# A graph layer's gathers through a circle of 8 pairs of row tiles in place of 35

## The chip, the cores and the metric

The kernel runs on one core of one Trainium2 chip. The metric is the device time of one execution in microseconds (us). TensorE is PE, VectorE is DVE, ScalarE is ACT, GpSimd is POOL, and SP is the engine that issues most of the plain DMAs. PE's weight loads are listed apart, as PEld.

## The reference

There are N = 3125 nodes with 128 features and 50000 edges, sorted by destination `dst`. Each edge has one of 16 types, each node one of 8.

```python
h   = relu(layernorm(x))
hW  = einsum('nd,tdf->tnf', h, W_edge) + b_edge[:, None, :]
msg = hW[etypes, src] / counts[dst, etypes]          # mean over the edges of one type at one node
agg = segment_sum(msg, dst)
hN  = einsum('nd,tdf->tnf', h, W_node) + b_node[:, None, :]
out = x + relu(hN[ntypes, arange(N)] + agg)
```

## The kernel before

The kernel first makes h for all nodes, splits it in two float16 halves and stores them as `h_table` in HBM, 25 blocks of 128 nodes. The edge weights are applied late: the kernel first sums h[src] over the edges of each (node, type), and then multiplies these sums by `W_edge`.

The 50000 edges are 391 tiles of 128, taken in 196 pairs of tiles (`PAIRS`). For each tile POOL issues one indirect DMA (line 390), the gather, which fetches the 128 rows h[src] from `h_table` into one slot of `G`. The second tile of every eighth pair is not gathered: PE makes it from the h that lies in SBUF with one-hot products (`pe_fetch`, line 276), and ACT puts it into `G` (line 283). So there are 368 gathers, 15 for each 8 pairs.

PE's `sums` takes a pair's two slots and multiplies them by one-hots of (type, destination) that DVE writes into `oh` (line 964): four matmuls of line 693, at whose end it raises `pair_mm`. DVE then adds the result into `S` (line 973). Each group of 8 pairs (`PPB`) completes one block of 128 nodes: DVE scales the sums by reciprocal counts (`dve_scale`, line 353), SP loads the next block's 1 MB of reciprocals (line 247), ACT zeroes (line 309), and PE multiplies by the weights of nodes and edges between its next pairs (lines 328 to 337).

POOL's order is its program. It issues the 6 gathers of the first three pairs (`LATE`), reads a flag, waits for `mask_ready`, which DVE raises after line 907, and then goes through the pairs. Ahead of each gather stands a wait that the gather three before it has landed (`NEAR`), and ahead of each pair from the 36th on a wait for `pair_mm`: the pair 35 before it must have been summed, since `G` is a circle of `BODY + LATE` = 35 pairs. The first 25 slots of `G` hold, until line 907 has read them, `nt_row`, the types of the nodes; that is why the wait for `mask_ready` stands there.

Before its sums, PE counts the edges of each (node, type) with 392 small matmuls (line 673), in turns with DVE (line 931) and ACT (line 592). Between its sixth and seventh pair it waits for a one-hot of DVE, which at that time joins the counts and takes their reciprocals (lines 990 to 998).

Of the kernel before, what the change touches and what calls it, by code (L numbers as in the profile page):

```python
# [25 lines left out]
def gnn_layer(nc, x, src, dst, etype, ntype, w_edge, b_edge, w_node, b_node, out):  # L26
# [18 lines left out]
    LATE = 3  # L45
    NEAR = 3
    BODY = 4 * PPB
    ITERS = (PAIRS - LATE) // BODY
    assert PAIRS - LATE - ITERS * BODY == 1 and NB == 4 * ITERS + 1 and R * W <= 512
    AHEAD = 128  # L50
    TURN = 8
    H_SCALE = 4096.0
    MID = NB * P // 2
# [19 lines left out]
    with ctx:  # L73
        def sb(name, shape, dt):
            return ctx.enter_context(nc.sbuf_tensor(name, shape, dt))
# [4 lines left out]
        def sem(name):  # L80
            return ctx.enter_context(nc.semaphore(name))
# [20 lines left out]
        src_t = sb("src_t", [P, TC], I32)  # L102
# [97 lines left out]
        mask_ready = sem("mask_ready")  # L200
# [8 lines left out]
        issuing = sem("issuing")  # L209
        landed = [sem(f"landed{m}") for m in range(TURN)]  # L210
        oh_ready = sem("oh_ready")
        pair_mm = sem("pair_mm")
# [68 lines left out]
        def act_fetch(act, b):  # L281
            act.wait_ge(fetch_mm, b + 2)
            nc.scalar.activation(G[:, 2 * slot_of(LATE + PPB * b + PPB - 1) + 1, :], misc[:, 0:2 * D],  # L283
                                 ACT.Copy).then_inc(fetched, 1)
# [88 lines left out]
            return got  # L373

        def slot_of(pair):
            return (pair + BODY) % (BODY + LATE)

        def is_fetched(pair, a):
            return a == 1 and pair != PAIRS - 1 and pair >= LATE and (pair - LATE) % PPB == PPB - 1

        def gathers_upto(pair, a):

            return 2 * pair + a - sum(is_fetched(p, 1) for p in range(pair))

        def wait_landed(engine, n):

            engine.wait_ge(landed[n % TURN], 16 * (n // TURN + 1))

        def gather(pool, slot, index, done):
            nc.gpsimd.indirect_dma_start(  # L390
                out=G[:, slot, :], out_offset=None, in_=h_table[:, :],
                in_offset=bass.IndirectOffsetOnAxis(ap=index, axis=0)).then_inc(done, 16)
# [67 lines left out]
        @block.gpsimd  # L460
        def _(pool):
            nc.gpsimd.memset(ones[:, :], 1.0)
            nc.gpsimd.memset(zcol[:, :], 0.0)
            nc.gpsimd.memset(id32[:, :], 0.0).then_inc(consts, 1)
            nc.gpsimd.memset(bias[:, :], 0.0).then_inc(consts, 1)
            pool.wait_ge(consts, 1)
            nc.gpsimd.affine_select(out=id32[:, :], in_=id32[:, :], compare_op=ALU.not_equal, fill=1.0,
                                    base=0, pattern=[[-1, P]], channel_multiplier=1).then_inc(consts, 1)
            pool.wait_ge(consts, 3)
            nc.gpsimd.tensor_copy(id16[:, :], id32[:, :]).then_inc(consts, 1)  # L470
            with nc.allow_low_precision(reason="integers up to 2048 are exact in float16"):
                nc.gpsimd.iota(iota[:, :], pattern=[[1, R * P + 1]], base=0, channel_multiplier=0,
                               allow_small_or_imprecise_dtypes=True)
            nc.gpsimd.iota(pair16[:, :], pattern=[[16, PAIRS]], base=0, channel_multiplier=0,
                           allow_small_or_imprecise_dtypes=True).then_inc(consts, 1)
            pool.wait_ge(consts, 5)
            nc.gpsimd.iota(kcol[32:64, :], pattern=[[0, 1]], base=0, channel_multiplier=1,
                           allow_small_or_imprecise_dtypes=True).then_inc(consts, 1)
            pool.wait_ge(consts, 6)
            nc.gpsimd.iota(node_col[:, :], pattern=[[P, NB]], base=-MID, channel_multiplier=1,  # L480
                           allow_small_or_imprecise_dtypes=True)
            nc.gpsimd.memset(S[:, :, :], 0.0).then_inc(zeroed_s, 1)
            nc.gpsimd.memset(bsel[0:64, :], 0.0).then_inc(zeroed_s, 1)

            pool.wait_ge(src_ready, 1)
            pool.wait_ge(h_stored, 16 * 5)
            for j in range(LATE):
                for a in range(2):
                    gather(pool, 2 * (BODY + j) + a, src_t[:, 2 * j + a:2 * j + a + 1],
                           landed[2 * j + a])  # L490
            pool.wait_ge(flag_ready, 1)
            bad = pool.value_load(flag[0:1, 0:1], min_val=0, max_val=FLAG_MAX)
            pool.wait_ge(mask_ready, 1)
            with pool.If(bad < 1):
                for n in range(2 * LATE - NEAR):
                    wait_landed(pool, n)
                for pair in range(LATE, PAIRS):
                    if pair >= LATE + BODY:

                        pool.wait_ge(pair_mm, pair - LATE + 1)  # L500
                    for a in range(2):
                        if not is_fetched(pair, a):
                            n = gathers_upto(pair, a)
                            wait_landed(pool, n - NEAR)
                            pool.sem_inc(issuing, 1)  # L505
                            gather(pool, 2 * slot_of(pair) + a, src_t[:, 2 * pair + a:2 * pair + a + 1], landed[n % TURN])
            with pool.Else():
                for s in range(0, NB, SEG):
                    with pool.Fori(0, min(SEG, NB - s) * NT) as n:
                        pool.wait_ge(g_src, s * NT + n + 1)  # L510
                        pool.sem_inc(issuing, 1)
                        gather(pool, 0, src_s[:, 0:1], g_rows[s // SEG])
                        pool.wait_ge(g_rows[s // SEG], (n + 1) * 16)
# [122 lines left out]
        def _(pe):  # L636
# [24 lines left out]
            with pe.If(bad < 1):  # L661
# [37 lines left out]
                for j in range(LATE):  # L699
                    if j == 2:  # L700
                        pe.wait_ge(c_out, 2 * CITERS + 1)
                    sums(j, j, slot_of(j), (j - LATE) % 4, 0)
# [65 lines left out]
        def _(dve):  # L768
# [108 lines left out]
            def in_range(cols, values, low, high):  # L877

                own(nc.vector.tensor_scalar(viol[:, cols], values, -0.5 * (low + high), 2.0 / (high - low + 1),
                                            ALU.add, ALU.mult))  # L880
            in_range(slice(0, V1 // 2), rel[:, 0:V1:2], 0, W0 - 1)
            in_range(slice(V1 // 2, V1), rel[:, 1:V1:2], 0, W - 1)
            in_range(slice(V1, V2), relq[:, :], 0, WQ - 1)
            in_range(slice(V2, V3), viol[:, V2:V3], -16 * LATE, AHEAD)
            in_range(slice(V3, V4), viol[:, V3:V4], WQ, 2 * N)
# [229 lines left out]
```

## Time and profile before

| what | value |
|---|---|
| median of 3 runs | 623.2 us (619.66 to 623.7) |
| time of the profiled execution | 623.44 us |
| its span in the trace | 621.5 us |
| mean granted clock of PE | 0.857 of full speed |
| gathers, their busy time on POOL | 368, 392.2 us |
| POOL idle just before a gather, in total | 198.3 us |

The span runs from the first instruction to the last; the profiled execution took 1.9 us more than its span. A gather's row on POOL is the making of its descriptors; its data land some us later.

### The profile page before, as it was taken

What the parts mean: (1) busy time and instruction counts of PE and PEld (TensorE: products, weight loads), DVE (VectorE), ACT (ScalarE), POOL (GpSimd) and SP (SyncE); (2) the same over time, 40 slices, a digit from 0 to 9 for tenths busy, and PEclk for the clock granted to TensorE, in tenths of its full rate; (3) what the DMA queues carried; (4) which work ended last, traced back from release to release, by engine and by line L of the source; (5) the groups of instructions that cost most, each with busy time, mean ns of one, the idle gap of its engine ahead of it and who ended that gap; (6) DMA issues with size and microseconds to landing.
All of it is one profiled execution on the core that took longest, in us unless ns stands there. A gap on an engine that the chain in (4) does not pass through costs nothing.

```text
span 621.5 us, 9756 instructions
## 1 busy us (share of the span) xinstructions
PE 434.3 (70%) x3143; PEld 351.9 (57%) x3143; DVE 363.0 (58%) x913; ACT 172.7 (28%) x402; POOL 405.8 (65%) x384
## 2 busy tenths in 40 slices
PE   0269849977786675776776776767766776776687
PEld 0169628865565563665564565555645564565477
DVE  5966778876635545645645545646545646545633
ACT  2922424423313303213203213213203203303300
POOL 8067775666765576766766765766766766776760
PEclk9755559997977977978987978988898978988979
DMA  5541154333323313223323223223223323323320
GB/s 149 147 108 51 38 165 163 120 117 111 111 64 112 114 51 104 74 91 119 91 80 109 78 89 114 81 90 111 87 83 112 90 81 112 104 64 116 112 55 13
DMA packets 32497, 60.35 MB, mean 97 GB/s; under 512 B 7416, under 2 KB 22836, under 8 KB 29236
## 3 DMA queue, kind: packets, MB, share of 16 engines
q1 hardware_dynamic: 19372, 34.83, 17.1%
q0 software_dynamic: 11776, 24.14, 14.2%
q10 hardware_dynamic: 1296, 0.71, 0.5%
q8 instruction: 28, 0.46, 0.3%
q14 instruction: 25, 0.20, 0.1%
HBM read 56.01 MB, written 3.65 MB: 96 GB/s over the span
## 4 chain that ended last, share of the span: by engine, by line
DMA 57%; issue 17%; PE 16%; POOL 6%; DVE 2%; ACT 1%; SPq 1%; POOLq 0%; DVEq 0%; ACTq 0%
DMA G<-h_table,src_t 56%; POOL G L390 6%; PE out_ps L337 6%; PE acc L693 5%; PE misc L276 2%; PE out_ps L328 1%; DMA xs<-in_x_dram 1%; ACT union_a L543 1%; SPq L402 1%; PE misc L337 1%; PE node_ps L317 0%; POOLq L505 0%; PE out_ps L330 0%; DVE bsel L907 0%; PE misc L328 0%
## 5 line engine op out<-in xcount | busy, mean ns | idle before, releaser
L390 POOL DMA_INDIRECT G<-h_table,src_t x368 | 392.2, 1066 | 198.3 <-DMA G<-h_table,src_t 113.6
L693 PE MATMUL acc<-oh,G 128*128 128x384 f16 (+1 forms) x784 | 148.7, 322 | 150.6 <-issue 83.5
L973 DVE TENSOR_TENSOR S<-S,acc 128x384 f32 x196 | 108.2, 552 | 207.5 <-PE acc L693 207.0
L693 PEld LDWEIGHTS acc<-oh,G 128*128 128x128 f16 x784 | 75.3, 105 | 214.1 <-issue 124.2
L337 PE MATMUL out_ps<-w_all,union_a 128*128 128x128 f32 x768 | 120.7, 324 | 0.0
L337 PEld LDWEIGHTS out_ps<-w_all,union_a 128*128 128x128 f32 x768 | 116.7, 240 | 0.8
L964 DVE TENSOR_SCALAR oh<-iota,seg 128x224 f16<-128x224 f16 (+1 forms) x396 | 102.7, 313 | 10.3 <-issue 10.3
L283 ACT ACTIVATE G<-misc 128x256 f16<-128x256 f32 x24 | 9.2, 384 | 317.4 <-PE misc L276 306.7
L276 PE MATMUL misc<-hh,union_c 128*128 128x256 f16 x600 | 79.5, 278 | 0.0
L276 PEld LDWEIGHTS misc<-hh,union_c 128*128 128x128 f16 x600 | 59.7, 100 | 6.2
L296 ACT ACTIVATE dg<-id,wmask 128x128 f16<-128x128 f16 x200 | 60.7, 386 | 0.0
L309 ACT ACTIVATE S<-zcol 128x2048 f32<-128x2048 f32 x23 | 43.9, 1909 | 59.1 <-DVE union_a L353 59.1
L353 DVE TENSOR_TENSOR union_a<-S,union_b 128x2048 f32<-128x2048 f32 (+1 forms) x25 | 56.1, 2243 | 0.9
L267 DVE TENSOR_TENSOR union_c<-src_r,union_d 128x1024 f16<-128x1024 f16 (+1 forms) x72 | 50.9, 707 | 2.5
L328 PE MATMUL out_ps<-w_all,hN 128*128 128x128 f32 x384 | 49.5, 284 | 0.0
L328 PEld LDWEIGHTS out_ps<-w_all,hN 128*128 128x128 f32 x384 | 47.3, 201 | 0.1
L673 PE MATMUL acc<-union_c 128*16 128x44 f16 x392 | 31.0, 256 | 6.9 <-DVE union_c L931 6.9
L673 PEld LDWEIGHTS acc<-union_c 128*16 128x16 f16 x392 | 30.8, 114 | 7.0 <-DVE union_c L931 7.0
L317 PE MATMUL node_ps<-dg,hh 128*128 128x512 f16 x100 | 27.1, 395 | 0.0
L304 ACT ACTIVATE hN<-node_ps 128x1024 f32<-128x1024 f32 x25 | 25.0, 1001 | 0.0
L641 PE MATMUL acc<-id,union_b 128*128 128x128 f32 x12 | 2.8, 423 | 17.1 <-DVE union_b L837 17.1
L317 PEld LDWEIGHTS node_ps<-dg,hh 128*128 128x128 f16 x100 | 10.2, 102 | 7.3 <-issue 1.1
(97 smaller groups left out, 171.1 us busy)
## 6 DMA issues: line engine op xcount, KB each, us to landing
union_b<-rc_table SPq DMA_DIRECT2D x25, 1024.0 KB, 4.8
G<-h_table,src_t POOLq DMA_INDIRECT x368, 2.6
h_table<-hh SPq DMA_DIRECT2D x5, 320.0 KB, 2.6
src_row<-in_src_dram SPq DMA_DIRECT2D x24, 64.0 KB, 2.9
out_dram<-os SPq DMA_DIRECT2D x24, 64.0 KB
xs<-in_x_dram SPq DMA_DIRECT2D x4, 320.0 KB, 5.1
w_all<-in_L_gnn_W_node_dram SPq DMA_DIRECT2D x1, 512.0 KB
xs<-in_x_dram SPq DMA_DIRECT2D x1, 256.0 KB
```

Of the source, the lines that this page charges most:

```text
L267: nc.vector.tensor_tensor(fetch[:, first:end, :], src_r16[:, p:p + 1, :].to_broadcast([P, end - first, P]), node_of[:, first:end, :], ALU. ...
L276: last = nc.tensor.matmul(misc[:, 0:2 * D], fetch[:, k, :], hh[:, k, :], start=(k == 0), stop=(k == NB - 1))
L296: last = nc.scalar.activation(dg[:, p, k, :], id16[:, :], ACT.Copy, scale=wmask[:, bass.ds(b, 1), k])
L309: nc.scalar.activation(S[:, :, r * P:(r + 1) * P], zeros3, ACT.Copy).then_inc(zeroed, 1)
L328: nc.tensor.matmul(into[0:rows, 0:D], hN[:, p, k, 0:rows], w_all[:, R + k, :], start=(k == 0), stop=False)
L337: last = nc.tensor.matmul(into[0:rows, 0:D], Sn[:, p, t, 0:rows], w_all[:, t, :], start=False, stop=(t == R - 1))
L353: nc.vector.tensor_tensor(Sn[:, p, :, 0:rows], S[:, :, r * P:r * P + rows], rcb[:, p, :, 0:rows], ALU.mult).then_inc(scaled, 1)
L390: nc.gpsimd.indirect_dma_start(out=G[:, slot, :], out_offset=None, in_=h_table[:, :], in_offset=bass.IndirectOffsetOnAxis(ap=index, axis=0 ...
L673: last = nc.tensor.matmul(bank[0:R, v * WQ:(v + 1) * WQ], tcnt[:, q, :, 4 * v + a], ncnt[:, q, :, 4 * v + a], start=(a == 0), stop=(a == 3))
L693: last = nc.tensor.matmul(window[:, :, 0:w], G[:, 2 * g_slot + a, part * D:(part + 1) * D], oh[:, o, a, 0:R * w].rearrange("p (t n) -> p t ...
L964: last = nc.vector.tensor_scalar(oh[:, o, a, 0:width], iota_w[:, 0:width], cols[:, a:a + 1], None, ALU.is_equal)
L973: nc.vector.tensor_tensor(span, span, acc[bank][:, 0:R * W].rearrange("p (t n) -> p t n", n=W), ALU.add).then_inc(s_add, 1)
```

## The change

`slot_of` puts the pairs into a circle of 8 (`SLOTS`), the last 8 of the 35 pairs of slots. POOL therefore waits, from the ninth pair on, until the pair 8 before it has been summed. Those slots don't overlap `nt_row`, and the wait for `mask_ready` moves into the other path (`Else`), which these inputs don't take. `G` keeps its size; the gathers, their order and the waits on landings stay.

```diff
+    SLOTS = 8
...
         def slot_of(pair):
-            return (pair + BODY) % (BODY + LATE)
+            return BODY + LATE - SLOTS + pair % SLOTS
...
-                    gather(pool, 2 * (BODY + j) + a, src_t[:, 2 * j + a:2 * j + a + 1],
+                    gather(pool, 2 * slot_of(j) + a, src_t[:, 2 * j + a:2 * j + a + 1],
                            landed[2 * j + a])
...
-            pool.wait_ge(mask_ready, 1)
             with pool.If(bad < 1):
...
-                    if pair >= LATE + BODY:
+                    if pair >= SLOTS:
-                        pool.wait_ge(pair_mm, pair - LATE + 1)
+                        pool.wait_ge(pair_mm, BODY + pair - SLOTS + 1)
...
             with pool.Else():
+                pool.wait_ge(mask_ready, 1)
```

(`pair_mm` starts at `BODY`, so both waits ask for a number of sums: pair - 34 and pair - 7.)

## Rows read from the trace of the kernel before

**Rows 1.** The page: the chain that ended last, by engine.
```profile
DMA 57%; issue 17%; PE 16%; POOL 6%; DVE 2%; ACT 1%; SPq 1%; POOLq 0%; DVEq 0%; ACTq 0%
```

**Rows 2.** Waits of PE, first 69 to 130 us, then 130 to 605: total, times, longest.
```profile
PE acc L693 <- DVE oh L964: 11.4, 2, 10.3
...
PE acc L693 <- issue: 83.5, 62, 4.4
PE acc L693 <- DMA G<-h_table,src_t: 55.3, 19, 6.1
```

**Rows 3.** Gathers on POOL in six stretches: busy (x gathers), PE clock, DMA share, GB/s.
```profile
30.00:54.90 24.90, 17.67 (x16) 0.50 0.37 98
54.90:70.60 15.70, 10.81 (x11) 0.50 0.19 49
70.60:87.60 17.00, 13.86 (x10) 0.60 0.30 71
87.60:128.40 40.80, 25.76 (x23) 0.94 0.48 161
128.40:587.60 459.20, 312.19 (x296) 0.88 0.30 94
587.60:605.00 17.40, 11.94 (x12) 0.80 0.33 110
```

**Rows 4.** Timeline of POOL, single gathers: start, duration, idle before and its releaser.
```profile
38.26 0.94 POOL L390 DMA_INDIRECT G<-h_table,src_t  x1 [0.30 <-issue]
40.69 0.94 POOL L390 DMA_INDIRECT G<-h_table,src_t  x1 [1.49 <-DMA G<-h_table,src_t]
...
53.38 1.30 POOL L390 DMA_INDIRECT G<-h_table,src_t  x1 [0.30 <-issue]
54.98 0.94 POOL L390 DMA_INDIRECT G<-h_table,src_t  x1 [0.30 <-issue]
...
65.60 0.94 POOL L390 DMA_INDIRECT G<-h_table,src_t  x1 [1.81 <-DMA G<-h_table,src_t]
...
70.65 0.95 POOL L390 DMA_INDIRECT G<-h_table,src_t  x1 [0.30 <-DMA G<-h_table,src_t]
...
73.16 5.36 POOL L390 DMA_INDIRECT G<-h_table,src_t  x1 [0.30 <-DMA G<-h_table,src_t]
...
604.03 0.95 POOL L390 DMA_INDIRECT G<-h_table,src_t  x1 [0.30 <-issue]
```

**Rows 5.** Timeline of PE, 69 to 91 us (a pair is four matmuls of L693).
```profile
69.27 3.20 PE L693 MATMUL acc<-oh,G 128*128 128x384 f16 x12 [1.11 <-DVE oh L964]
...
73.97 2.27 PE L693 MATMUL acc<-oh,G 128*128 128x384 f16 x12
86.51 2.19 PE L693 MATMUL acc<-oh,G 128*128 128x384 f16 x8 [10.28 <-DVE oh L964]
...
90.41 1.22 PE L693 MATMUL acc<-oh,G 128*128 128x384 f16 x4
```

**Rows 6.** Timeline of DVE: mask input, add of the first pair, joining the counts.
```profile
32.21 1.88 DVE L907 TENSOR_SCALAR bsel<-G,kcol 8x3200 f32<-8x3200 int32 x1
...
70.57 0.55 DVE L973 TENSOR_TENSOR S<-S,acc 128x384 f32 x1
...
73.07 3.47 DVE L990 TENSOR_TENSOR union_b<-union_b,union_a 16x3200 f32<-16x3200 f32 x1
76.58 1.81 DVE L993 TENSOR_SCALAR bsel<-union_b 16x3200 f32<-16x3200 f32 x1
```

**Rows 7.** Timeline of PE, the same place in two groups of 8 pairs.
```profile
98.26 1.21 PE L693 MATMUL acc<-oh,G 128*128 128x384 f16 x8
...
111.91 1.21 PE L693 MATMUL acc<-oh,G 128*128 128x384 f16 x8
```

**Rows 8.** Waits of POOL, 130 to 605 us.
```profile
POOL G L390 <- DMA G<-h_table,src_t: 96.9, 146, 3.7
POOL G L390 <- issue: 49.2, 152, 2.5
POOL G L390 <- PE acc L693: 6.3, 9, 2.4
```

**Rows 9.** The page: gathers, median us from issue to landing.
```profile
G<-h_table,src_t POOLq DMA_INDIRECT x368, 2.6
```

## The prediction

> **What bounds the kernel now.** I read the chain that ended last first: 57% of it is DMA, nearly all of it the landing of gathers, and PE has 16% [rows 1]. That names the gathers, but not whether their data or their issue sets the pace, nor from when. The waits of PE answer when: from 69 to 130 us it waits only for one-hots of DVE, 11.4 us in all; from 130 to 605 us its waits are for landed gathers, 55.3 us, and for something that the profile can't name, 83.5 us, and none for DVE [rows 2]. So PE begins with rows to spare and has used them up by about 130 us.
>
> Next the pace of POOL, as gathers in stretches [rows 3]. By 128.4 us it has issued 16 + 11 + 10 + 23 = 60 of 368; then 296 more take 459.2 us, 1.551 us each, or 23.3 us for the 15 of a group. Undisturbed, two gathers start 1.25 us apart: 0.94 us of work and 0.30 us between [rows 4]. Fifteen would take 18.75 us, so each group carries 4.5 us of disturbance: gathers stretched while DVE scales a block, and waits for the landing of the third gather before while the 1 MB of reciprocals come in. The waits of POOL have the size of it [rows 8]. PE alone does 8 pairs with all work between them in 111.91 - 98.26 = 13.65 us [rows 7]. POOL needs 23.3 us for what PE does in 13.65 us: the string of gathers, begun at about 30 us and ended at 604.03 us [rows 3, 4], is the bound, and what follows it, to the span's end at 621.5 us, is a fixed tail of 17.5 us. PE's head start in rows is spent by 130 us and never comes back. Hence the rule for the sum: any us that POOL stands still before its last gather is a us at the end, unless that us would have been lost to POOL anyway.
>
> **The new wait.** Pairs 1 to 8 have 16 gathers, and POOL has issued these 16 by 54.9 us: the 16th starts at 53.38 [rows 3, 4]. The 17th started at 54.98. With 8 pairs of slots it needs the sum of the first pair. PE begins that at 69.27 us and does three pairs in 3.20 us [rows 5]; DVE, which waits for the same signal, starts its add at 70.57 [rows 6]. With the usual step between signal and gather, POOL resumes at about 70.8. Nothing in the change brings PE forward here: it is counting until then, in turns with DVE and ACT, and uses no gathered row. The stall is 70.8 - 54.98 = 15.8 us. Queued behind the waiting instruction on POOL are all 352 gathers that are left; for them waits PE.
>
> **What the stall swallows.** The 11 gathers that POOL made in 54.9 to 70.6 us [rows 3] now come after it. There they had taken 70.65 - 54.98 = 15.67 us, 1.92 us above 11 x 1.25 = 13.75, chiefly the idle 1.81 in place of 0.30 before the gather at 65.60 [rows 4]. What disturbs the string later is tied to blocks (scaling, reciprocals), of which there are as many as before; so the 11 are priced bare, at 13.75 us. Resuming at 70.8 one place where 27 gathers stood at 70.65: +0.15. Together +13.9 us.
>
> **Is there a second stall?** From 70.8 on, each pair asks for the one 8 before it. Sums of pairs 1 to 6 are over by 76.24 us, pair 7 begins at 86.51 [rows 5]. POOL now makes the 11 gathers of pairs 9 to 14. One of them will fall on DVE's joining of counts (73.07 to 78.4) and be held as that at 73.16 was, 5.36 us in place of 0.94 [rows 4, 6]. The 11 so end at 70.8 + 13.75 + 4.4 = 88.95 us, and then pair 15 asks for pair 7, over at about 87.7 [rows 5]: no wait. If the gather weren't held, POOL would be there at 84.5 and wait until 88.0: 0.9 us sooner than with the hold, no more. So either way the string stands at 88 to 89 us with 27 gathers issued, where it stood at 87.6 with 37 [rows 3]. Check: 10 gathers are missing, 12.5 us, and 1.3 us of clock, 13.8 in all. From there PE ends pairs faster than POOL asks (pair 9, begun at 90.41, is asked for at about 94 us). The cover of that step is PE's pace; were PE's seventh pair x us later than 87.7 + 1.2, the end would be x us later.
>
> **Who misses the rows.** In 87.6 to 128.4 us, while PE was fast, 23 gathers took 40.8 us, 1.77 each [rows 3]. At that pace the 40th gather, the last one of the 21st pair, starts at 88.95 + 12 x 1.77 = 110.2 and lands 2.6 us later [rows 9], at 112.8, while PE would be at that pair at 111.91 [rows 7]. So PE overtakes there, and no longer near 130 us, and from there on each group runs at 23.3 us. The 23 gathers stood 12 us above bare, with three blocks in them: 4.0 each, against 4.5 in the long stretch. One to one and a half groups change from the one to the other: +0.5 us.
>
> **The wait for the mask.** It goes, and gives nothing: line 907 ended at 34.09 us [rows 6], while POOL's seventh gather, behind that wait, started at 40.69, held by the first landings and the flag's reading [rows 4]. And even a us won here would only lengthen the stall at the 17th gather, whose end PE sets. **More waits.** 27 more pairs carry a wait for `pair_mm`. The gathers step by 1.25 us both where pairs had none (before the 36th) and where they had one, so it hides in the 0.30 us between gathers; the steps agree to 0.01 us, which bounds it by 0.3 us in all. **Smaller circle.** PE, DVE and the transfers see other addresses of the same memory, no other work; nothing in a row ties a duration to the slot, so nothing either way. ACT's write of the fetched tile goes where the pair 8 before was, which PE summed before it made that tile: no new wait.
>
> **The sum.** 13.9 + 0.5 = 14.4 us on the profiled execution's 623.44: 637.8 us. That execution stands 0.2 us above the median of 623.2, which doesn't matter here. Ends for the unknown parts: if each of the 11 moved gathers cost the mean of the long stretch, 1.551, they take 17.1 us, and with 0.15 + 0.5 + 0.3 for the waits it is +18.0: 641.5. With no hold at 73 us (-0.9), no change of pace (-0.5) it is +13.0: 636.4; and the runs of before reach 3.6 us below their median. I take the bare price since what disturbs POOL comes once a block, not once a gather.
>
> **Where two rules speak.** The row shows that a gather beside DVE's joining lasted 5.36 us [rows 4, 6]. The Trainium skill (SBUF — State Buffer, section SBUF: two separate sides) says that GpSimd can't write descriptors while DVE holds the port pair they share; the trace agrees with the 4.4 us. By that rule a POOL that stands still loses nothing to DVE, and a stall would be partly free. But the stall ends at 70.8, before DVE's long instructions start at 73.07, so here the rule would take nothing from the sum. The Trainium skill (Perfetto Trace Analysis, section Optimization Strategy) also holds that a gap that repeats on an engine can mean too few buffers; by it the circle of 8 would be felt in every group, which is the second rival below.
>
> **Rivals.** *The stall is absorbed (no change).* If PE were the bound later on, it would make up for the rows that come late. Against it: PE's 13.65 us a group against POOL's 23.3, and 138.8 us of PE's waits after 130 us. It would need the long stretch to lose 8 us or more of its 459.2 - 296 x 1.25 = 89 us of disturbance by a lucky shift of phase. Time 623 to 629; chance 0.04.
>
> *A wait in every group (much slower).* POOL is bound to PE's sums in the long stretch too. Each of 24 groups would get one wait of the size of the longest that POOL's rows lay to PE, 2.4 us [rows 8]: 24 x 2.4 = 58, with the stall 696 us. It decides from the point at which POOL is 8 pairs ahead of PE's last full sum. Against it: PE waits for rows from 130 us on, so POOL is one to two pairs ahead there, far from 8; the 6.3 us of PE in POOL's waits can't be the circle's, at a distance of 35. Chance 0.02.
>
> *Gathers step aside (faster).* If POOL, held by the slots, stood still exactly while DVE scales a block, the stretching of gathers would go. A gather of the long stretch is busy for 312.19 / 296 = 1.055 us in place of 0.94 [rows 3], 1.7 us a group: 24 x 1.7 = 41 us off 638 gives 597 us; it turns the sign from 0.6 us a group on. Place: the group's last pair. For it: the disturbances are 89 us in the long stretch alone. Against it: it needs a full circle at every block, and the circle is nearly empty when PE is starved. Chance 0.03.
>
> *The stall is other than 15.8.* If PE's restart at 86.51 slips or more gathers meet DVE's long instructions in 73 to 86 us, some us come on top, as one more hold of 4.4 us would: 642.2. This is in the range.
>
> **How the numbers follow.** The forecast has 0.91, the rivals 0.04, 0.02 and 0.03. Range 632.5 to 643: the low end is the sum's low end less the 3.6 us of run to run, the high one the bound of the dear gathers, 641.5, and 1.5 us for a slip of the restart. 1% is 6.2 us, about what a measurement of this kernel can tell from no change; faster 0.03, same 0.05 (the absorbed case and a stall that is half hidden), slower 0.92.
>
> **What the profile after would show.** POOL: 16 gathers by about 54.9 us, then one idle time of near 15.8 us with PE's line 693 as its releaser, the next gather at 70.6 to 71. PE: sums from 69.3 us on as before, restart at 86.5. POOL at 27 gathers at 88 to 89 us. PE's first wait for gathers near 112 us in place of 130. In the long stretch 1.55 us a gather, and the last gather at 618.4, with 17.5 us behind it. The prediction is wrong if PE's sums start well before 69 us once POOL is silent, if a second idle time of POOL shows before 90 us, or if the pace of the long stretch moves: 1% of 459 us is 4.6 us, more than any other doubt in the sum.

## The result and the profile after

The kernel with the circle of 8 takes 635.84 us (635.07 to 636.62) against 623.11 us (619.66 to 623.7): +12.7 us, ratio 1.0219, 95% interval 1.0187 to 1.0251. (Medians and ranges are of all runs; ratios leave out a run that is over 1.5% above the fastest of its kernel.) The profiled execution has a span of 633.5 us, 12.0 us more than before, and lines are numbered one higher from line 51 on.

The chain that ended last, on the page of the changed kernel, by engine and then by line:

```profile
DMA 57%; PE 20%; issue 13%; POOL 5%; DVE 2%; ACT 1%; SPq 1%; POOLq 0%; DVEq 0%; ACTq 0%
DMA G<-h_table,src_t 55%; PE acc L694 5%; POOL G L391 5%; PE acc L674 5%; PE out_ps L338 4%; PE out_ps L329 2%; PE misc L277 2%; DMA xs<-in_x_dram 1%; ACT union_a L544 1%; PE misc L338 1%; SPq L403 1%; PE out_ps L331 0%; POOLq L505 0%; DVE bsel L908 0%; PE misc L329 0%
```

By engine it says nearly nothing [rows 1]. By line it has one thing that the page before had not: PE's counting (line 674), 5% or 31 us, behind which POOL now stands. But the page of the circle of 16, which lost nothing, has these 5% too, so the chain shows a place and no price. The stretches of POOL's gathers, columns as in [rows 3], show where the time went:

```profile
30.00:54.90 24.90, 17.25 (x16) 1.00 0.37 100
54.90:70.60 15.70, 0.00 (x0) 1.00 0.02 5
70.60:88.00 17.40, 13.69 (x11) 0.75 0.30 70
88.00:144.00 56.00, 36.76 (x34) 0.90 0.41 140
144.00:600.00 456.00, 312.61 (x298) 0.89 0.31 93
600.00:617.00 17.00, 11.50 (x12) 0.80 0.32 105
```

Sixteen gathers by 54.9 us as before, then none where there had been 11, then 11 by 88 us. The whole loss of gathers is made in the second row. The timeline of POOL at the stall, and its last gather, which answer to [rows 4]:

```profile
53.19 0.94 POOL L391 DMA_INDIRECT G<-h_table,src_t  x1 [0.30 <-issue]
71.27 0.94 POOL L391 DMA_INDIRECT G<-h_table,src_t  x1 [17.13 <-PE acc L694]
72.51 0.94 POOL L391 DMA_INDIRECT G<-h_table,src_t  x1 [0.30 <-PE acc L694]
73.76 4.76 POOL L391 DMA_INDIRECT G<-h_table,src_t  x1 [0.31 <-issue]
...
87.61 1.26 POOL L391 DMA_INDIRECT G<-h_table,src_t  x1 [0.30 <-issue]
89.17 1.25 POOL L391 DMA_INDIRECT G<-h_table,src_t  x1 [0.30 <-DMA G<-h_table,src_t]
...
615.92 0.94 POOL L391 DMA_INDIRECT G<-h_table,src_t  x1 [0.30 <-issue]
```

One idle time of 17.13 us with PE's sums as its releaser; DVE's hold is still there, on the 19th gather instead of the 30th; the 28th gather, which is the first to need PE's seventh pair, comes without a wait. PE's timeline, to be held against [rows 5], hardly moved up to its restart:

```profile
69.28 3.18 PE L694 MATMUL acc<-oh,G 128*128 128x384 f16 x12 [1.01 <-DVE oh L965]
...
86.42 2.19 PE L694 MATMUL acc<-oh,G 128*128 128x384 f16 x8 [11.54 <-DVE oh L965]
...
107.13 0.68 PE L694 MATMUL acc<-oh,G 128*128 128x384 f16 x4 [1.48 <-issue]
...
111.04 0.68 PE L694 MATMUL acc<-oh,G 128*128 128x384 f16 x4 [0.98 <-DMA G<-h_table,src_t]
...
118.11 2.19 PE L694 MATMUL acc<-oh,G 128*128 128x384 f16 x8 [4.18 <-issue]
```

Before, PE had waited for no gather until about 130 us. Here only the row at 111.04 names a landing. But the idle time before the row at 107.13 ended 0.09 us after the last gather of that pair had landed (started at 104.58, landed 2.46 us later), and so did the 4.18 us before 118.11 (started at 111.17, landed 6.85 us later). So PE's first waits for gathers lie at 107 to 111 us, and some of what the profile puts down to "issue" is a wait for a landing.

### The profile page after: what moved, and what is told of

Same layout as the page of the kernel before. It is cut to its first block, busy times and chain, and to the rows that moved or that the text cites. A ratio compares the mean times of both kernels' runs of the same rounds, so it can differ in the third digit from the quotient of the medians.

```text
span 633.5 us, 9756 instructions
## 1 busy us (share of the span) xinstructions
PE 433.1 (68%) x3143; PEld 351.0 (55%) x3143; DVE 363.9 (57%) x913; ACT 172.7 (27%) x402; POOL 405.4 (64%) x384
## 4 chain that ended last, share of the span: by engine, by line
DMA 57%; PE 20%; issue 13%; POOL 5%; DVE 2%; ACT 1%; SPq 1%; POOLq 0%; DVEq 0%; ACTq 0%
DMA G<-h_table,src_t 55%; PE acc L694 5%; POOL G L391 5%; PE acc L674 5%; PE out_ps L338 4%; PE out_ps L329 2%; PE misc L277 2%; DMA xs<-in_x_dram 1%; ACT union_a L544 1%; PE misc L338 1%; SPq L403 1%; PE out_ps L331 0%; POOLq L505 0%; DVE bsel L908 0%; PE misc L329 0%
## 5 line engine op out<-in xcount | busy, mean ns | idle before, releaser
L694 PEld LDWEIGHTS acc<-oh,G 128*128 128x128 f16 x784 | 73.9, 104 | 228.5 <-issue 135.2
L277 PE MATMUL misc<-hh,union_c 128*128 128x256 f16 x600 | 77.7, 274 | 0.0
L318 PE MATMUL node_ps<-dg,hh 128*128 128x512 f16 x100 | 25.7, 379 | 0.0
```

Source lines behind the costliest of these rows:

```text
L277: last = nc.tensor.matmul(misc[:, 0:2 * D], fetch[:, k, :], hh[:, k, :], start=(k == 0), stop=(k == NB - 1))
L694: last = nc.tensor.matmul(window[:, :, 0:w], G[:, 2 * g_slot + a, part * D:(part + 1) * D], oh[:, o, a, 0:R * w].rearrange("p (t n) -> p t ...
```

## The experiments

All are made from one of the two kernels by the lines shown. Each ran beside the kernel before; its times there are given. The first four take the change apart and ran in one series (before: 621.99 us, 617.14 to 627.21).

**One wait alone.** The circle keeps 35 pairs; a single wait is added.

```diff
                 for pair in range(LATE, PAIRS):
+                    if pair == 8:
+                        pool.wait_ge(pair_mm, BODY + 1)
```

> The kernel before, circle of 35, with a single added wait: ahead of the 9th pair POOL waits for the sum of the first pair. Theory one (the whole loss is that one stall of POOL): the time of the changed kernel again, 634 to 638 us, one idle time of POOL of 16 to 17 us at the 17th gather. Theory two (the small circle itself also acts in the long stretch, for better or worse): the long stretch differs from that of the changed kernel, and the time with it by 4 us or more.

Measured: 639.86 us (632.75 to 643.15), ratio 1.0277 (1.0159 to 1.0396); the four runs are 632.75, 637.76, 641.95 and 643.15. The profiled execution, 637.76 us, has the stall of the changed kernel to the hundredth:

```profile
54.67 0.94 POOL L390 DMA_INDIRECT G<-h_table,src_t  x1 [0.30 <-issue]
72.74 0.94 POOL L390 DMA_INDIRECT G<-h_table,src_t  x1 [17.13 <-PE acc L695]
```

(Everything in it comes some 1.4 us later, from the first gather on.) The median is 2 us above the expected range and the runs spread widely: the interval allows a loss of 10 to 25 us, in which the 12.7 of the changed kernel lies. So one wait is enough for a loss of that size, and the remaining 187 waits and the eight pairs of slots aren't needed for it.

**The distance of 8 everywhere but at the start.** From the kernel before:

```diff
                     if pair >= LATE + BODY:
-                        pool.wait_ge(pair_mm, pair - LATE + 1)
+                        pool.wait_ge(pair_mm, BODY + pair - 8 + 1)
```

> The kernel before, circle of 35 in memory, but from the 36th pair on POOL asks for the sum of the pair 8 before instead of 35 before; the first 35 pairs run free. Theory one: no idle time of POOL comes of it, 620 to 625 us. Theory two: 5 us or more from the time before, on either side.

Measured: 619.24 us (616.18 to 624.33), ratio 0.9998 (0.9958 to 1.0037). That is 0.8 us below the expected range and short of the 5 us of theory two. Asking for the pair 8 before costs nothing over 161 pairs, within some 2.5 us. POOL's waits there, over the whole span, columns as in [rows 8]:

```profile
POOL G L390 <- DMA G<-h_table,src_t: 108.6, 166, 3.4
POOL G L390 <- issue: 66.8, 189, 3.9
...
POOL G L390 <- PE acc L693: 4.8, 11, 0.8
```

The 4.8 us in 11 waits put down to PE are mostly the usual 0.30 us between gathers, with PE's signal as the last to come. So the start carries the loss, and the distance of 8 later on carries none that these runs can see.

**The wait for the mask put back.** From the changed kernel:

```diff
             bad = pool.value_load(flag[0:1, 0:1], min_val=0, max_val=FLAG_MAX)
+            pool.wait_ge(mask_ready, 1)
             with pool.If(bad < 1):
...
             with pool.Else():
-                pool.wait_ge(mask_ready, 1)
```

> The changed kernel with the wait for the mask put back where it was. Theory one: nothing, 635 to 637 us, the seventh gather starts within 0.2 us of 40.8. Rival (the moved wait gave back part of the loss): 637 to 640 us.

Measured: 637.93 us (634.02 to 640.03), ratio 1.0298 (1.0244 to 1.0352). The median lies 0.9 us inside the range of the rival, the runs reach over both ranges, and the interval touches that of the changed kernel (1.0187 to 1.0251), so the times don't decide; the trace does. The seventh gather starts at 40.62 us, no later than in the changed kernel (40.79), the 17th at 71.2 us, the last at 614.66. So the wait at its old place held nothing up, and what it could hold up stands ahead of the stall, whose end PE sets.

**A circle of 16.** From the changed kernel, `SLOTS = 16`.

> The changed kernel with a circle of 16 pairs. Its first 31 gathers are free, and the 32nd came at 80.1 us in the kernel before, after the first sum's end at 70.5. Theory one: no stall at all, 621 to 625 us. Theory two: some of the 12.7 us stays, 626 us or more.

Measured: 621.5 us (617.21 to 625.02), ratio 0.9994 (0.9959 to 1.0029). No stall: 39 gathers are issued by 88.5 us, where the kernel before had 38 and the changed one 27. The smaller memory, the other addresses and the waits of 180 pairs are free, within some 2.5 us.

**A circle of 12 and a circle of 4.** From the changed kernel, `SLOTS = 12` and `SLOTS = 4`. Their first runs, with two more, were made on a chip on which the kernel before took 701.67 us (674.09 to 720.43); they say nothing of the sizes and stand further down. The second runs, beside 621.37 us (618.74 to 624.28):

> The circle of 12 once more, since in its first run PE's counting was broken up (sums begun at 85.6 us in place of 69.3) and the kernel before itself took 674 to 720 us beside it. Theory one, where the kernel before takes 617 to 627 us: 4 gathers fewer at 70.8 us, +5.2 us, 626 to 630 us. If PE's counting is broken up again while POOL issues gathers and runs freely while POOL stands, that is a cost of gathers beside counting that the first chip did not have.

Measured: 627.98 us (625.62 to 629.59), ratio 1.0101 (1.0071 to 1.0131): +6.6 us for 4 gathers fewer. The idle time before the 24th gather:

```profile
63.15 0.94 POOL L391 DMA_INDIRECT G<-h_table,src_t  x1 [0.30 <-issue]
71.46 0.94 POOL L391 DMA_INDIRECT G<-h_table,src_t  x1 [7.37 <-PE acc L694]
```

> The circle of 4 once more. Theory one: 19 gathers fewer at 70.8 us, some of DVE's hold and of the restart on top, +25 us, 645 to 652 us; 1.53 to 1.56 us a gather in the long stretch. Theory two (the circle of 4 binds in every group): over 655 us.

Measured: 647.17 us (645.79 to 653.66), ratio 1.0414 (1.0366 to 1.0461): +25.8 us for 19 fewer, 28.19 us of idle time before the ninth gather. POOL's stretches to 144 us and the long one:

```profile
30.00:70.60 40.60, 9.34 (x8) 0.50 0.19 51
70.60:89.00 18.40, 14.61 (x11) 0.59 0.30 69
89.00:144.00 55.00, 35.25 (x34) 0.79 0.37 120
144.00:595.00 451.00, 304.44 (x290) 0.88 0.31 94
```

451 us for 290 gathers is 1.555 us each, the pace of the kernel before. Even a circle of 4 costs no pace once PE is starved. (The profiled execution is the slowest of the five, 653.66 us.)

The four sizes on one line, by gathers issued at 88.5 us (before 38; circles of 12, 8, 4: 34, 27, 19): 4, 11 and 19 gathers fewer, +6.6, +12.7 and +25.8 us, or 1.65, 1.16 and 1.36 us each. They lie around the undisturbed step of 1.25, above it more than below; with errors of 2 to 3 us on each time, any price from 1.2 to 1.4 us fits all three.

**Five gathers in flight.** The runs point to what really sets the pace: POOL waiting for landings. From the kernel before, `NEAR = 5`, the circle of 35.

> Five gathers in flight, circle of 35, once more. If PE's counting runs undisturbed: about 2 us off each group, 575 to 600 us. If five in flight starve PE's counting on any chip (it got one matmul each 2.8 us while POOL issued): sums begun only when the circle of 35 is full, near 115 us or later, and 650 us or more.

Measured: 561.76 us (559.22 to 565.06), ratio 0.9026 (0.8964 to 0.9087): 60 us faster, more than expected, and faster than both kernels of this study. POOL's waits over the span:

```profile
POOL G L390 <- issue: 70.4, 231, 0.3
POOL G L390 <- DMA G<-h_table,src_t: 37.2, 118, 1.0
```

In the kernel before, 113.6 us in 162 waits were put down to landings; now it is 37.2 us in 118, 0.3 us each, the mere step between gathers. Above that step it is 2 us for 65, and those 63 us are about the gain. In the long stretch a gather takes 1.386 us, against 1.555 before. The expectation of 2 us a group (48 us) was too small by the rest.

**Five in flight and the circle of 8.** From the changed kernel, `NEAR = 5`; beside it the kernel before took 621.62 us.

> Five gathers in flight with the circle of 8 pairs. Five in flight with 35 pairs took 561.8 us and had issued 41 gathers when, at 89.2 us, the circle of 8 will have issued 27, as the changed kernel did: the first stall and DVE's hold don't depend on the depth. Theory one (the cost is the gathers forgone by then, each at the undisturbed step): 14 x 1.25 = +17.5 us, 579 us (576 to 582), more than the 12.7 us that the same circle cost with three in flight. Rival (the cost is the idle time, the same whatever the depth): +12 to 13 us, 574 us. Where PE's counting is broken up by gathers, as in the runs beside which the kernel before took 674 to 720 us, it tells nothing of this.

Measured: 581.5 us (576.87 to 584.73), ratio 0.9331 (0.9275 to 0.9387), so +19.7 us against five in flight with 35 pairs, run in another series; from the ends of the two intervals the difference may be as small as 12. The traces are sharper:

```profile
51.33 1.31 POOL L391 DMA_INDIRECT G<-h_table,src_t  x1 [0.30 <-issue]
71.31 0.94 POOL L391 DMA_INDIRECT G<-h_table,src_t  x1 [18.67 <-PE acc L694]
```

By 88.5 us 27 gathers are issued against 41, and the last one starts at 562.36 us against 543.12: +19.2. Fourteen gathers forgone at 1.25 us are 17.5 us. This speaks for the gathers forgone as what sets the cost, by which a faster string of gathers makes the same circle dearer; the times alone don't exclude the rival's 12 to 13 us.

**The four runs on the other chip.** For the circles of 12 and 4:

> The changed kernel with a circle of 12 pairs: 23 gathers (24 less the one that PE makes) are free, the next stood at 65.6 us before and now waits to about 71. Four gathers fewer by 70.8 us. Theory one: 4 x 1.25 + 0.2 = +5.2 us, 628 us (626 to 630). If the loss were the idle time and not the gathers left to do, about the same here; if it were a property of the small circle, nearer to 635.

> The changed kernel with a circle of 4 pairs: 8 gathers are free, then POOL stands from about 43 to 71 us, 28 us, and has 19 gathers fewer done at 70.8. Theory one: the ones left are made up at 1.25 us each until the restart of PE at 86.4, 12 of them; the pair after that needs PE's seventh pair. 19 x 1.25 + 0.2 + 1 to 2 for DVE's hold at 73 us = +25 us, 648 us (645 to 652), and 1.53 to 1.55 us a gather in the long stretch, where POOL is one to two pairs ahead. Theory two (the circle binds in every group): over 655 us.

For five in flight, with 35 and with 16 pairs:

> The kernel before with 5 gathers in flight in place of 3 (each waits for the landing of the fifth before it). If POOL's waits for landings beside the 1 MB loads are disturbance that more depth hides: about 2 us off each of 24 groups, 575 to 590 us. If the transfers or the making of descriptors set the pace there: 615 to 625 us.

> Five gathers in flight and a circle of 16 pairs. The same as five in flight with 35 pairs, within 3 us, if only the stall at the first sums makes the circle matter: with the gathers faster, the 32nd comes at some 76 us, still behind the first sum at 70.5.

Measured there: 680.88 us (677.05 to 685.31), 695.99 us (693.95 to 697.64), 696.96 us (695.51 to 697.93) and 672.76 us (671.38 to 674.57), against 701.67 us of the kernel before, whose own runs reach from 674.09 to 720.43. None came as theory one had it (the circle of 4 lies over 655 us, where theory two was to be, but there the kernel before lies over it too), and no ratio is drawn from so wide a base. Five in flight with 16 pairs was not run again elsewhere. PE's counting shows something that no other run has. Timeline of PE with five in flight, 35 pairs:

```profile
98.62 0.23 PE L673 MATMUL acc<-union_c 128*16 128x44 f16 x1 [2.56 <-issue]
101.42 0.23 PE L673 MATMUL acc<-union_c 128*16 128x44 f16 x1 [2.56 <-issue]
104.23 0.24 PE L673 MATMUL acc<-union_c 128*16 128x44 f16 x1 [2.57 <-issue]
...
124.59 23.93 PE L673 MATMUL acc<-union_c 128*16 128x44 f16 x302 [0.47 <-issue]
149.53 3.20 PE L693 MATMUL acc<-oh,G 128*128 128x384 f16 x12 [1.01 <-DVE oh L964]
```

PE's first 56 counting matmuls ran in one piece to 42 us. From 46 to 107 us, while POOL issues gathers, PE does one small matmul each 1.4 to 2.8 us and waits in between for nothing that the profile names. POOL fills its circle and stops at 114.2 us; from 124.59 us PE does 302 matmuls in 23.93 us. The same kernel on the chip of its second run did all 392 in one piece:

```profile
37.27 31.02 PE L673 MATMUL acc<-union_c 128*16 128x44 f16 x392 [6.89 <-DVE union_c L931]
69.30 0.99 PE L693 MATMUL acc<-oh,G 128*128 128x384 f16 x3 [1.01 <-DVE oh L964]
```

The other three runs of that chip fit: with the circle of 4 POOL stands from 43 us and counting is in one piece, sums from 69.40 us; with 12, POOL stands from 62.8 and the counting is free from 66.82, sums from 85.62; with 16 and five in flight, sums from 102.55 us. So on that chip a small circle spares PE's counting. But that isn't all that was slow there: the circle of 4, with its counting whole, still took 49 us more than on the chip of its second run. The pages of these four runs put 29 to 39% of the chain that ended last down to "another core or an unknown queue", which stands on no page of the other chips:

```profile
another core or an unknown queue 34%; PE 21%; DMA 13%; ACT 10%; issue 9%; DVE 9%; POOL 1%; DVEq 1%; SPq 1%; POOLq 0%; ACTq 0%
```

(circle of 4.) And the string of gathers isn't the bound there, at least in three of the four. After the last gather come 71.3 us with five in flight and 35 pairs, 37.5 with 16, 36.7 with the circle of 12 and 19.8 with that of 4, in place of 17.5; and where elsewhere POOL, from 130 us on, has at most 4 pairs begun that PE hasn't summed (three in flight), here it fills its circle now and then: at 3 of its gathers with 12 pairs, at 7 with 35 and at 25 with 16. The kernel before has no trace there. What PE lacks in those gaps (its instructions, or something else), and whether it was the chip or the hour, stays open.

## Why the prediction was right

**The bound.** Right. The string of gathers ends the kernel: from the last gather to the end of the span it is 633.5 - 615.92 = 17.6 us, 17.5 before. Five in flight is the proof from the other side: a faster string alone takes 60 us off.

**The new wait.** Right in place and kind, the 17th gather, one stall. POOL resumed at 71.27 us and not at 70.8: DVE's add, released by the same signal, started at 70.59, and POOL's gather 0.68 us behind it, where I had put 0.2, a step that no row showed. The idle time was 17.13 us for the 15.8 that I gave: 0.5 is this later signal, 0.3 the step that stands before every gather and that I had left out of the idle time, and 0.55 that the gather before it ended earlier, at 54.13 us for 54.68. That PE isn't brought forward was right too: its sums began at 69.28 us with POOL silent.

**What the stall swallows, and the second stall.** Right: no second stall. I put the 28th gather at 88.95 us; it started at 89.17. The later start of 0.5 us was half made up by DVE's hold, 4.76 us in place of 5.36. In both traces the held gather ended at 78.52 us, 0.13 us after DVE's two instructions that begin at 73.07. The Trainium skill's account of that hold (SBUF — State Buffer, section SBUF: two separate sides) fits: the hold moved to whichever gather DVE met, and the stall, over before DVE's long instruction began at 73.07 us, escaped none of it.

**Who misses the rows.** PE's first waits for gathers came at 107 and 111 us for 112. The 40th gather started at 111.17 us for 110.2, but it landed 6.85 us later, not the median of 2.6, so that the 21st pair began at 118.11 us. The rate in that part was mis-sized a little: between the two traces the gathers of the same number lie 15.5 us apart at the 76th, for 14.4 forecast.

**The sum.** 14.4 us forecast, 12.7 by the medians, 12.0 by the spans. The term that was off is the pace of the long stretch, held constant in the sum: 298 gathers in 456.0 us are 1.530 us each against 1.551 [rows 3], which gave back some 4 us by the end: the gathers of the same number lie 15.5 us apart at the 76th and 11.9 at the last, which started at 615.92 us for the 618.4 forecast. A moved pace, by 1% of the stretch, was one of the signs of being wrong that I had named. It moved by 1.4% in these stretches and by 0.9% between the same gathers, so that the forecast still held is in part luck. I don't find that it comes from the circle: between the 61st and 361st gather the kernels with three in flight run at 1.555 (before), 1.541 (changed), 1.533 (mask put back), 1.539 (one wait), 1.533 (35 pairs, late distance 8), 1.539, 1.553 and 1.556 us (12, 4 and 16 pairs), in no order of size. With one profile of each it isn't shown what it does come from. A change of 0.02 us a gather is 6 us over these 300, more than any other doubt, as I had said. The two other kernels with the same stall came out at +15.9 and +17.9 us by their medians, so, as an estimate from the three, the cost lies at 12 to 18 us and the forecast within it. (A slip in the range: 636.4 less 3.6 is 632.8, not 632.5, which changes nothing.)

**The rivals.** Absorbed: refuted by the time, and by the circle of 4, whose loss grows with the gathers forgone. A wait in every group: refuted by the late distance of 8 and by the pace of the circle of 4; the Trainium skill's rule on repeated gaps and buffers (Perfetto Trace Analysis, section Optimization Strategy) that stood behind it doesn't fit here: the gaps that repeat in every group came from the number of gathers in flight, not from slots. Gathers step aside: refuted, the gathers are held as before, 312.61 / 298 = 1.049 us each against 1.055.

## What to carry to other kernels

Don't ask how far a producer is ahead on average, but where its lead is built: here a consumer that is starved for 500 us leaves two to three pairs of slots in use on average and four at most (pairs whose gathers POOL has begun and PE has not yet summed, counted at each gather from 130 us on), yet for the first 40 us, while it did something else, 12 pairs weren't enough and 16 were. The cost of too few slots was the number of items forgone by the time the consumer started, times roughly the producer's undisturbed step (1.2 to 1.7 us each here, for 1.25), and it counts only if the producer is the bound at the end. And where a queue's waits are for its own landings, try more in flight before more slots: here it was worth 60 us, and slots beyond 16 pairs nothing.

## What the runs showed of the hardware

Three gathers of 128 rows in flight run at 1.53 to 1.56 us each beside 1 MB loads, five at 1.38 to 1.39, against an undisturbed step of 1.25.

Part of the disturbance has a plain form. Of the 23 gathers that start beside DVE's scaling of a block in the trace of the kernel before (line 353, 2.29 us, two float32 inputs in SBUF), 22 end 0.81 to 0.83 us after that instruction, whenever they started. DVE's instruction and one such gather:

```profile
109.96 2.29 DVE L353 TENSOR_TENSOR union_a<-S,union_b 128x2048 f32<-128x2048 f32 x1
...
110.87 2.20 POOL L390 DMA_INDIRECT G<-h_table,src_t  x1 [0.30 <-issue]
```

In the changed kernel's trace two gathers that start within 0.01 us of such an instruction are not held and last 0.95 us.

The granted clock of PE didn't show in the time: in the counting before the first sums it was 1.00 in the changed kernel's trace and 0.50 in that of before, and the sums began at 69.28 and 69.27 us. Of the 19 runs of the kernel before in the first series, the five with a mean clock below 0.87 took 617.14 to 622.95 us, the 14 with 0.88 and more 617.62 to 627.21.

On one chip, PE's counting took 48, 64 and 111 us in three of four runs in place of 31, while POOL issued gathers; no run on the other chips showed this.
